# Attention values with the tokens on the partitions, and five transform stages on 64x64 tiles of TensorE, in a fused attention and convolution kernel

## The reference

```python
# block 1: windowed attention and MLP, 1024 tokens of 128 channels
t = layernorm(tok)                       # into 16 windows of 64 tokens
q, k, v = t @ qkv_w.T + qkv_b            # 8 heads of 16
attn = softmax(q * hd**-0.5 @ k.T + bias)
out = attn @ v
tok = tok + out @ proj_w.T + proj_b
tok = tok + gelu(layernorm(tok) @ w1.T + b1) @ w2.T + b2
# block 2: convolutions, gates and a spectral branch
out0 = gelu(conv1x1(x))
x_fca = abs(ifft2(fft2(out0) * x_att))
x_sca = conv1x1(gap(x_fca)) * x_fca
x1, x2 = conv1x1(x_sca), conv1x1(x_sca)
spectral = abs(ifft2(x1 * (fft2(x2) * (1 + boost * mask)))) * alpha + x_sca * beta
out = x + gates(out0) * (7-tap and 3x3 depthwise, dilated 3x3 group convs) + spectral
return conv1x1(relu(out))
```

## Time and profile before

| | |
|---|---|
| median of 3 runs | 1524.92 us (1521.01 to 1527.33) |
| profiled execution | 1529.35 us, of which the span of the trace 1527.6 us |
| TensorE matmuls, weight loads | 1404.7 us (92%), 847.3 us (55%) |
| VectorE | 1321.4 us (87%) |
| ScalarE | 955.9 us (63%) |
| GpSimd | 408.7 us (27%) |
| granted clock of TensorE | 0.975 of 2.4 GHz in the mean |

### The profile page before, as it was taken

The page is one execution under the profiler, slowest core; times in us unless marked ns, Lnnn a source line. Parts: engine busy times, 40 slices in busy tenths (PEclk is TensorE's granted clock), DMA queues, the critical chain, the costliest instruction groups (busy, mean ns, idle before and its releaser), DMA issues.

```text
span 1527.6 us, 37499 instructions
## 1 busy us (share of the span) xinstructions
PE 1404.7 (92%) x14384; PEld 847.3 (55%) x14384; DVE 1321.4 (87%) x2312; ACT 955.9 (63%) x1717; POOL 408.7 (27%) x316
## 2 busy tenths in 40 slices
PE   5679999999999999999999999999999999999984
PEld 3346656465565646556564655656465565746552
DVE  4628898989989899998989989898989989898867
ACT  3364856667575666757566675756658575674633
POOL 3005050320505023050502305051230604024060
PEclk9789999999999999999999999999999999999997
DMA  4102012130201213020121302012130211212020
GB/s 164 26 14 67 13 33 72 17 89 15 64 29 35 72 17 89 15 64 29 32 76 17 89 15 64 29 32 76 17 89 14 54 40 32 62 17 76 1 64 28
DMA packets 32604, 70.65 MB, mean 46 GB/s; under 512 B 14116, under 2 KB 17188, under 8 KB 32068
## 3 DMA queue, kind: packets, MB, share of 16 engines
q1 hardware_dynamic: 32452, 68.28, 17.7%
HBM read 22.41 MB, written 9.08 MB: 21 GB/s over the span
## 4 chain that ended last, share of the span: by engine, by line
DVE 42%; DVEq 17%; PE 16%; ACT 15%; issue 8%; SPq 2%; DMA 1%; ACTq 0%
DVE hv L1189 15%; ACT fft L1502 6%; DVEq L1060 5%; DVE row_max L1061 4%; PE bank L743 4%; DVEq L1072 3%; DVE score L1063 3%; PE bank L547 2%; DVE inverse L1071 2%; PE bank L610 2%; ACT nT L1488 2%; ACT probT L1545 2%; ACT fft L1662 2%; DVEq L1106 2%; DVE score L1058 1%
## 5 line engine op out<-in xcount | busy, mean ns | idle before, releaser
L743 PE MATMUL bank<-act,mats_sb 128*32 128x512 f32 (+16 forms) x2592 | 221.0, 430 | 0.0
L1189 DVE SCALAR_TENSOR_TENSOR hv<-ver,mix,hv 128x1024 f32<-128x1024 f32 x144 | 184.9, 1284 | 10.8
L1875 POOL TENSOR_TENSOR resT<-qC,proj_shift 128x1024 f32<-128x1024 f32 x16 | 38.0, 2378 | 527.7 <-DVE x1T L1081 522.5
L1189 DVE SCALAR_TENSOR_TENSOR hv<-hor,mix,hv 128x1024 f32<-128x1024 f32 x128 | 164.4, 1285 | 10.9
L506 PE MATMUL bank<-cons_sb,fft 128*128 128x128 f32 x1280 | 161.1, 279 | 11.3 <-ACT fft L1502 10.1
L1502 ACT ACTIVATE fft<-bank 128x512 f32<-128x512 f32 x224 | 162.6, 802 | 12.2 <-PE bank L506 7.4
L506 PEld LDWEIGHTS bank<-cons_sb,fft 128*128 128x128 f32 x1280 | 148.8, 192 | 23.2 <-ACT fft L1502 14.3
L1895 POOL TENSOR_SCALAR hor<-act,cols_sb 128x1024 f32<-128x1024 f32 x16 | 25.0, 1565 | 488.3 <-ACT act L1579 426.3
L743 PEld LDWEIGHTS bank<-act,mats_sb 128*32 128x32 f32 x2592 | 125.5, 111 | 50.5 <-issue 30.2
L547 PE MATMUL bank<-k_heads,qC 128*64 128x512 f32 x512 | 142.0, 634 | 10.2 <-DMA k_heads<-kC 8.4
L1540 ACT ACTIVATE score<-score 128x512 f32<-128x512 f32 x128 | 80.1, 632 | 109.6 <-DVE score L1063 108.9
(11 more groups left out here) (184 smaller groups left out, 2690.8 us busy)
## 6 DMA issues: line engine op xcount, KB each, us to landing
pyr_stack<-pyr SPq DMA_DIRECT2D x96, 144.2 KB, 2.5
x_in<-x_dram SPq DMA_DIRECT2D x16, 512.0 KB, 4.9
k_heads<-kC SPq DMA_DIRECT2D x128, 64.0 KB, 2.5
edge<-edge_dram SPq DMA_DIRECT2D x16, 512.0 KB, 4.1
out_dram<-y_out SPq DMA_DIRECT2D x16, 512.0 KB, 3.4
k_heads<-rel_dram SPq DMA_DIRECT2D x2, 1024.0 KB, 13.2
mats_sb<-mats_dram SPq DMA_DIRECT2D x1, 1978.5 KB, 7.3
pyr_stack<-pyr SPq DMA_DIRECT2D x16, 123.2 KB, 2.3
```

What stands on the lines that cost most here:

```text
L743: last = pe.matmul(to, w_pyr[:, d, t], act[:, y0 + dy:y1 + dy, x0 + dx:x1 + dx], start=(t == 4), stop=(t == PYR_ORDER[8]), skip_group_chec ...
L1189: last = dve.scalar_tensor_tensor(hv[:], src, mix[:, a, k:k + 1], hv[:], ALU.mult, ALU.add)
```

## The change

*Values.* The probabilities become the stationary operand and the values the moving one, so that the tokens are on the partitions of the result. `v_pair` gets a seventeenth column of ones behind each head's 16 channels, which gives the sum of the probabilities in the same matmul: one matmul for each group of two heads and window, 8 of 34 columns, in place of 8 of 64 columns and 4 of 128. The reciprocal is then one value for each token and head (128x8), and its product goes to a new tile `attn_tok`. Since `project` needs the channels on the partitions, a new transpose on TensorE (`value_turn`) and a new copy on ScalarE (`value_copy`) follow, two slots later.

*Stages.* `multiply_tiles` takes the place of `multiply4` in the five stages: it uses that the constants are block-diagonal, and does each chunk in four matmuls of 64x64 by 64 columns on the four quarters of the array. The two halves are now the partitions 0 to 63 and 64 to 127 of the source, each into its own bank, done almost together at the end; the stage begins when both halves of its input are there. The copies behind it read the new order.

*Order.* Behind the slots `last_odd` stands between the turns of pairs 6 and 7 and ahead of `next_turns(i, f, 1)`, and ScalarE's `square_odd` and `x_copy(f, 1)` are moved.

```diff
+            def multiply_tiles(first_bank, src, weights, done, first=None):
+                pe.sem_inc(pe_turns)
+                for c in range(CH):
+                    for q in range(2):
+                        part = slice(64 * q, 64 * q + 64)
+                        rhs = (first if first is not None and c == 0 else weights)[part, part]
+                        for m in range(2):
+                            last = pe.matmul(bank[first_bank + q][64 * m:64 * m + 64, 64 * c:64 * c + 64],
+                                             src[part, c * P + 64 * m:c * P + 64 * m + 64], rhs, start=True, stop=True)
+                        if c == CH - 1:
+                            last.then_inc(done, 1)
             def values(i, j):
                 pe.wait_ge(pT_sb, 8 * i + j + 1)
                 if j >= 2:
-                    pe.wait_ge(o_scaled, 8 * i + j - 1)
+                    pe.wait_ge(oT_sb, 8 * i + j - 1)
                 ps = bank[(1, 3)[j % 2]]
-                for e in range(2):
-                    w = 2 * j + e
-                    for g in range(HP):
-                        pe.matmul(ps[32 * g:32 * g + 32, e * WT:(e + 1) * WT],
-                                  v_pair[:, w, g].rearrange("p e d -> p (e d)"),
-                                  probT[:, j % 2, g, e * WT:(e + 1) * WT], start=True, stop=True)
                 for g in range(HP):
-                    last = pe.matmul(ps[32 * g:32 * g + 32, P:2 * P], con("pair"),
-                                     probT[:, j % 2, g], start=True, stop=True)
+                    for e in range(2):
+                        last = pe.matmul(ps[64 * e:64 * e + 64, VW * g:VW * g + VW],
+                                         probT[:, j % 2, g, e * WT:(e + 1) * WT],
+                                         v_pair[:, 2 * j + e, g].rearrange("p e d -> p (e d)"), start=True, stop=True)
                 last.then_inc(o_ps, 1)
+            def value_turn(i, j):
+                pe.wait_ge(o_scaled, 8 * i + j + 1)
+                pe.transpose(bank[(1, 3)[j % 2]][:, 3 * P:4 * P], attn_tok[:, j % 2], ident).then_inc(oT_ps, 1)
             def project(i, k, f=None):
-                pe.wait_ge(o_scaled, 8 * i + 4 * k + 4)
+                pe.wait_ge(oT_sb, 8 * i + 4 * k + 4)
...
             def dft_rows(n):
-                for k in range(2):
-                    pe.wait_ge(x2_sb, 2 * n + k + 1)
-                    pe.wait_ge(pyr_sb, 2 * n + k + 1)
-                    multiply4(bank[4 + k], fa, k, con("dft_h")).then_inc(h_ps, 1)
+                pe.wait_ge(x2_sb, 2 * n + 2)
+                pe.wait_ge(pyr_sb, 2 * n + 2)
+                multiply_tiles(4, fa, con("dft_h"), h_ps)
...
             def scale_values(i, j):
 
                 dve.wait_ge(o_ps, 8 * i + j + 1)
-                ps = bank[(1, 3)[j % 2]]
-                dve.reciprocal(inverse[:, j % 2], ps[:, P:2 * P])
-                dve.drain()
-                dve.tensor_tensor(attn_out[:, P * j:P * j + P], ps[:, 0:P], inverse[:, j % 2], ALU.mult)\
+                ps = bank[(1, 3)[j % 2]][:, 0:HP * VW].rearrange("p (h d) -> p h d", d=HD + 1)
+                dve.reciprocal(inverse[:, j % 2], ps[:, :, HD])
+                dve.drain()
+                dve.tensor_tensor(attn_tok[:, j % 2].rearrange("p (h d) -> p h d", d=HD), ps[:, :, 0:HD],
+                                  inverse[:, j % 2].unsqueeze(2).broadcast_to([P, HEADS, HD]), ALU.mult)\
                    .then_inc(o_scaled, 1)
...
+            def value_copy(i, j):
+                act_.wait_ge(oT_ps, 8 * i + j + 1)
+                act_.activation(attn_out[:, P * j:P * j + P], bank[(1, 3)[j % 2]][:, 3 * P:4 * P], ACT.Copy)\
+                    .then_inc(oT_sb, 1)
```

More of the change, by code:

```diff
@@ L42 @@
 HP = HEADS // 2
+VW = 2 * HD + 2
 FF = 512
@@ L77 @@
     ("ident", P), ("dft_h", P), ("dft_w0", P), ("dft_w", P), ("even0", P),
-    ("even", P), ("odd0", P), ("odd", P), ("idft_h", P), ("high", CH), ("iota", 2), ("pair", 2 * HD))
+    ("even", P), ("odd0", P), ("odd", P), ("idft_h", P), ("high", CH), ("iota", 2))
 def shape_constants():
@@ L136, in shape_constants @@
     put("iota", np.stack([np.arange(P), np.arange(P) + P], 1))
-    put("pair", np.repeat(np.eye(2), [WT, WT], 0).repeat(HD, 1))
     return c.astype(np.float32)
@@ L290, in swin_conv_kernel @@
         o_ps = sem("o_ps")
+        oT_ps = sem("oT_ps")
+        oT_sb = sem("oT_sb")
         proj_ps = sem("proj_ps")
@@ L802, in inverse_even @@
             def inverse_even(n):
-                for k in range(2):
-                    pe.wait_ge(ge_sb, n + 1)
-                    pe.wait_ge(w_sb, 2 * n + 2)
-                    multiply4(bank[6 + k], fc, k, con("even"), con("even0")).then_inc(ae_ps, 1)
+                pe.wait_ge(ge_sb, n + 1)
+                pe.wait_ge(w_sb, 2 * n + 2)
+                multiply_tiles(6, fc, con("even"), ae_ps, con("even0"))
             def inverse_odd(n):
-                for k in range(2):
-                    pe.wait_ge(go_sb, 2 * n + k + 1)
-                    multiply4(bank[4 + k], fd, k, con("odd"), con("odd0")).then_inc(ao_ps, 1)
+                pe.wait_ge(go_sb, 2 * n + 2)
+                multiply_tiles(4, fd, con("odd"), ao_ps, con("odd0"))
             def turn_even(n):
@@ L823, in last_even @@
             def last_even(n):
-                for k in range(2):
-                    pe.wait_ge(te_sb, 2 * n + k + 1)
-                    multiply4(bank[6 + k], fc, k, con("idft_h")).then_inc(be_ps, 1)
+                pe.wait_ge(te_sb, 2 * n + 2)
+                multiply_tiles(6, fc, con("idft_h"), be_ps)
             def last_odd(n):
-                for k in range(2):
-                    pe.wait_ge(to_sb, 2 * n + k + 1)
-                    multiply4(bank[4 + k], fd, k, con("idft_h")).then_inc(bo_ps, 1)
+                pe.wait_ge(to_sb, 2 * n + 2)
+                multiply_tiles(4, fd, con("idft_h"), bo_ps)
             def out_conv(n):
@@ L925, in both @@
                     values(i, j)
+                value_turn(i, 6)
+                last_odd(n)
+                value_turn(i, 7)
                 if f is not None:
                     next_turns(i, f, 1)
-                last_odd(n)
                 project(i, 1)
@@ L1671, in row_spectrum_copy @@
                     act_.wait_ge(h_ps, 2 * n + k + 1)
-                    copy(other_order(fb, k), rows_of(bank[4 + k])).then_inc(h_sb, 1)
+                    copy(other_tile(fb, k), tile_rows(bank[4 + k])).then_inc(h_sb, 1)
             def spectrum_turn_copy(n):
@@ L1688, in inverse_odd_copy @@
                     act_.wait_ge(ao_ps, 2 * n + k + 1)
-                    copy(other_order(fb, k), rows_of(bank[4 + k])).then_inc(ao_sb, 1)
+                    copy(other_tile(fb, k), tile_rows(bank[4 + k])).then_inc(ao_sb, 1)
             def turn_even_copy(n):
@@ L1762, in swin_rest @@
                     prob_copy(i, j)
-                    if j >= 6:
-                        x_copy(f, j - 6, 8 - j)
+                    if j >= 2:
+                        value_copy(i, j - 2)
+                    if j == 6:
+                        x_copy(f, 0, 2)
                     if j + 2 < PAIRS:
                         exponent(i, j + 2)
+                value_copy(i, 6)
+                value_copy(i, 7)
+                x_copy(f, 1, 1)
                 deviation2(i, 0)
@@ L1794, in both @@
                             to_windows(f)
-                        elif j >= 6:
-                            x_copy(f, j - 6, 8 - j)
+                        elif j == 6:
+                            x_copy(f, 0, 2)
                     if j + 2 < PAIRS:
                         exponent(i, j + 2)
+                value_copy(i, 6)
+                square_odd(n)
+                value_copy(i, 7)
+                if f is not None:
+                    x_copy(f, 1, 1)
                 deviation2(i, 0)
                 normalise2(i, 0)
-                square_odd(n)
                 deviation2(i, 1)
@@ L1859, in _ @@
             pool.memset(v_pair[:], 0.0)
+            pool.drain()
+            for e in range(2):
+                pool.memset(v_pair[64 * e:64 * e + 64, :, :, e, HD:HD + 1], 1.0)
+            pool.drain()
             pool.wait_ge(onehot_ready, 4)
```

29 lines of the change are left out of this document (21 added, 8 removed).

## The result

The changed kernel takes 1537.4 us (median, 1529.5 to 1542.9) against 1525.5 us of the kernel before beside it: 1.0081 times as long, 95% interval 1.0062 to 1.0099. It is **slower by 0.8%**; I had forecast 1520 us, hardly a change, and given "slower" a chance of 0.33. The profiled execution took 1532.6 us, with a mean granted clock of 0.978; executions at 0.972 to 0.975 took 1537 to 1543.

What follows compares the result with a forecast made beforehand. It took ScalarE's run up to the square roots, then VectorE, to bound a pass. 15 passes x 0.15 us and both ends gave -4 us: 1529.4 to 1525 profiled, 1521 against the median, forecast 1520; range 1490 to 1552.

Steps and rivals of the forecast that it cites:

- The prices: Times assumed for single operations: reciprocal 0.25 us, values 0.55 to 0.58, value copy 0.25, turn 0.11, stage 1.1.
- rival 2: Transform stages: tiles that differ in rows don't run side by side, a stage takes 2.0 us, kernel 1557; chance 0.15.
- Step C: From ScalarE's last probability copy to the first square root of the second layer norm, which comes about 0.3 us later.
- Step D: Second square root, no longer behind `square_odd`: 0.15 us earlier, and with it VectorE's long run.
- Steps A and B: Pass up to ScalarE's run, then that run: it begins 1.2 us earlier, its last probability copy starts 0.7 earlier.
- the sum: 15 passes x 0.15 = 2 us, 2 to 3 us in the first image's attention, last image 0.5 later: together -4 us.
- step A: Pass up to 602.74 us: reciprocals saved on VectorE bring `boosted` 0.5 us and the start of ScalarE's run 1.2 earlier.
- That last part: Pass from about 618 us: VectorE leads, taps back to back until the next pass, at most 0.74 us of waiting.
- 1 (the savings come through): Whole pass falls to what TensorE holds, 3 to 4 us less, 1470 us; chance 0.15 with half-way cases 1490 to 1505.
- Rival 3: Value copies at 0.41 us and TensorE's semaphore increment at 0.2 are dear: 1533, up to 1540 us; chance 0.20.

Runs made afterwards that it cites:

- e6: The changed kernel with one wait added: GpSimd's first operation of an image waits for the sums behind VectorE's gate; 1500.2 us, 0.9837.
- e9: The kernel before with one wait added: GpSimd's first operation of an image starts behind VectorE's gate; 1509.3 us, 0.9889.
- e4: The changed kernel with another order behind the slots: last value turn ahead of the last inverse stage, square root ahead of its squares; 1492.8 us, 0.9790.
- e11: The changed kernel with both GpSimd's wait of e6 and the order behind the slots of e4; 1487.2 us, 0.9743.

## Why the prediction was wrong

**The prices were right.** The reciprocal takes 0.20 to 0.21 us (0.25 predicted), its product 0.29, the values 0.59 (0.55 to 0.58), a value copy 0.28 (0.25). VectorE is busy for 75.6 us in the pass (some 76), and its waits before `scale_values` and `rstd` are 3.5 and 2.4 us (5 together). Only the turn is dearer in one place, 0.25 us from its start to that of `last_odd` (0.11). TensorE behind the slots:

```profile
613.09 0.66 PE L587 MATMUL bank<-v_pair,probT 128*64 128x34 f32 x16 [0.56 <-ACT attn_out L1579]
...
613.93 1.16 PE L521 MATMUL bank<-cons_sb,fft 64*64 64x64 f32 x64
615.03 0.33 PE L594 MATMUL bank<-cons_sb,attn_tok 128*128 128x128 f32 x1
```

From 613.93 to 615.03 a stage takes 1.10 us, 17 ns a record, as forecast: rival 2 is out, tiles that differ in rows do run side by side.

**Step C had the right row of operations.** ScalarE, and VectorE with the first square root and the second:

```profile
612.08 0.69 ACT L1574 ACTIVATE probT<-bank 128x512 f32<-128x512 f32 x1
...
614.04 0.28 ACT L1579 ACTIVATE attn_out<-bank 128x128 f32<-128x128 f32 x1 [1.10 <-PE bank L594]
615.13 1.08 ACT L1703 ACTIVATE fft<-bank 128x512 f32<-128x512 f32 x2 [0.81 <-PE bank L521]
616.10 0.28 ACT L1579 ACTIVATE attn_out<-bank 128x128 f32<-128x128 f32 x1
616.26 0.62 ACT L1503 ACTIVATE qC<-bank 128x512 f32<-128x512 f32 x1
616.89 1.28 ACT L1512 ACT_TABLE_LOAD   x1
618.19 0.30 ACT L1512 ACTIVATE std<-mv,eps 128x4 f32<-128x4 f32 x1
```

```profile
618.52 0.18 DVE L1063 RECIPROCAL rstd<-std 128x4 f32<-128x4 f32 x1 [2.06 <-ACT std L1512]
...
621.42 0.18 DVE L1063 RECIPROCAL rstd<-std 128x4 f32<-128x4 f32 x1 [0.36 <-ACT std L1512]
621.68 0.56 DVE L1065 SCALAR_TENSOR_TENSOR shift<-mv,rstd 128x4 f32<-128x4 f32 x1
```

It is the row of operations I had written down, value copy, squares when `last_odd` is done, and then value copy, copy, table load and square root without a gap. From the copy of the last probabilities to the square root it takes 6.11 us, where 4.86 were needed before; I had said 5.8.

**Step D was right.** The two `rstd` stand 2.90 us apart, before 3.29 in most passes: the second is 0.39 nearer to the first, 0.45 by my two numbers.

**Steps A and B and the sum** can be tested only with the seam mended. In e6 against e9, from the start of `in_conv` and in the mean of 12 passes, ScalarE's run begins at 42.4 us for 43.9 (1.55 earlier, 1.2 forecast), the last `prob_copy` at 53.0 for 54.2 (1.15 earlier, 0.7 forecast), the first square root 0.1 later (0.3 forecast), the second `rstd` 0.28 earlier (0.15 forecast). A pass gains 0.4 us for 0.15, the kernel 9 us for 4: the path was right, its size was not.

**The step that failed** is the beginning of step A. For everything ahead of `row_spectrum_copy`, 29 us of the pass, it counts one reciprocal, 0.70 us earlier, and puts the order in which the engines enter the pass at nothing: neither the lead of TensorE over VectorE, nor GpSimd, nor TensorE's clock has a term. In the changed kernel ScalarE's run begins not 1.2 us earlier but 44.1 us behind `in_conv` in the passes without the fall of the clock and 45.7 in those with it, where e6 has 42.4 and the undisturbed pass 42.5. From there on the passes are alike: the second `rstd` comes 20.0 us later in all of them, and the next `in_conv` another 25.6 to 25.9. So the sentence "That last part is untouched by the change" holds, but the next one, "A pass therefore gets shorter only by as much as `norm2(i, 0)` and `norm2(i, 1)` come earlier", does not: TensorE now enters every pass but one with the large lead, and GpSimd, which I had left out of the argument as an engine with 27% to do, goes with TensorE and takes the ports first. The price is 1.63 us a pass (89.65 for 88.02) in 13 passes, and 1.65 more in the 6 with the half clock: 31 us by these numbers. At the end of VectorE's statistics the last row above shows a small case of the same: `shift` takes 0.56 us for 0.17 and ends at 622.24, 0.02 behind the end of GpSimd's `resT` (619.82 to 622.22 by its record, which is rough); that one I have not tested.

One row was also misread. "Its longest wait is 1.1 us" takes the total of two waits for one; the longest is 0.7. Nothing in the sum hangs on it.

Linked to it is the **pass chosen**. Of the before's 14 passes I read one, 558 to 647 us, and it was one of the 8 without the long wait. One line of the waits, 10 times and up to 2.1 us, would have shown that passes differ, and that the kernel stood at the edge: 6 on one side, 8 on the other. The rival that I lacked is then plain: "the six become thirteen", 7 passes x 1.65 and 2 falls of the clock x 1.65, 15 us on top of the sum. That is 1535 as an estimate, and 1537.4 was measured. The measured time lies inside my range (1490 to 1552), but the upper end stood there for rival 2, which did not happen: that it holds the time is luck.

Of the rivals, 1 (the savings come through) did not happen in this order of the tail; with the other order e4, at 1492.8, is one of its half-way cases, and e11, at 1487.2, goes a little beyond them. Rival 3's bounds on the value copy and the increment did not decide anything.

## What to carry to other kernels

Read several passes of a loop, not one: where the longest wait of a line stands in some of them and not in others, the kernel is at an edge, and a change that makes one engine earlier can tip it. Where GpSimd and VectorE work on the same image, write down which of them starts first at each seam, and if it matters, fix it with a wait; here one added wait on the engine with most slack was worth 16 us before and 37 after. A change that takes work off an engine can cost more than it saves, once through what it triggers and once more through TensorE's clock; after such a change the order of the last steps is tuned again before the change is judged.

## What the runs showed of the hardware

- Of a VectorE and a GpSimd operation on SBUF that overlap, the second to start is held: in the kernels before and after the gate takes 1.9 to 2.1 us for 1.23, or GpSimd's first operation 1.7 to 2.2 for 1.13. `batt_wide` ends 0.09 us behind GpSimd's operation (0.27 alone, 0.40 or 1.08 beside it).
- TensorE's granted clock fell to half behind 1.7 us of idle time in 5 of 14 passes, behind 2.1 in 6 of 13 (before in 4 of 6), behind 4.8 in all 14, behind 0.5 and 0.75 in none. One fall costs 1.4 to 1.7 us; the 28 products take 3.9 to 4.4 us for 2.71 behind it.
- Four tiles of 64x64 run side by side: 64 records in 1.10 us, 17 ns a record, where two tiles take 31.6 ns a record.
